# A mixture-of-experts kernel on one core: fixed row regions per expert, a two-part scatter and wide logit products

## What is computed

```python
h = tok(x)                                   # patches @ proj.T + bias + position
h = h + attn(_layernorm(h), ...)             # state-space block
h = h + ffn(_layernorm(h), gate_w, w1, w2, w3, ws1, ws2, ws3)

def ffn(x, ...):                             # T = 1024, D = 192, HID = 512, E = 8, TOP_K = 2
    logits = xf @ gate_w.T
    scores = softmax(logits)
    topk_w, topk_idx = top_k(scores, 2)
    topk_w = topk_w / (topk_w.sum(-1, keepdims=True) + 1e-20)
    cw = zeros((T, E)).at[arange(T)[:, None], topk_idx].add(topk_w)
    y = zeros_like(xf)
    for e in range(E):
        y = y + cw[:, e:e + 1] * _ffn(xf, w1[e], w2[e], w3[e])
    return y + _ffn(xf, ws1, ws2, ws3)       # _ffn(t, a, b, c) = silu(t @ a.T) * (t @ c.T) @ b.T
```

## Time and profile before

| | us |
|---|---|
| three runs, median | 367.04 |
| three runs, lowest and highest | 366.01, 369.85 |
| the profiled execution | 368.0 |
| its span, first to last instruction | 366.3 |

### The profile page before, as it was taken

How to read it: one execution, slowest core, us unless ns; L and a number is a source line. 1 busy time by engine, 2 the same in 40 slices (tenths; PEclk the granted TensorE clock), 3 DMA queues, 4 the chain that set the end, 5 groups by cost and what they waited for, 6 DMA issues and landing times.

```text
span 366.3 us, 6306 instructions
## 1 busy us (share of the span) xinstructions
PE 330.1 (90%) x2042; PEld 270.4 (74%) x2043; DVE 239.3 (65%) x365; ACT 194.1 (53%) x331; POOL 204.2 (56%) x162
## 2 busy tenths in 40 slices
PE   5699979999998788799769999989999999999990
PEld 5653756847876676688668988878888888888870
DVE  1366997989998999999997588864332332223320
ACT  1146993957995666685916649952222222222220
POOL 8120287687896999898875327720333333333332
PEclk9999996999999999899979689999999999999997
DMA  7990820000023320410899999262223322222212
GB/s 188 238 329 17 337 123 2 2 1 5 0 113 118 116 115 4 115 45 2 187 199 233 292 215 236 92 140 70 52 51 52 48 45 45 40 47 50 36 21 22
DMA packets 30184, 37.01 MB, mean 101 GB/s; under 512 B 6112, under 2 KB 26128, under 8 KB 29136
## 3 DMA queue, kind: packets, MB, share of 16 engines
q1 hardware_dynamic: 24160, 30.84, 31.6%
q0 software_dynamic: 4080, 4.39, 7.1%
q10 hardware_dynamic: 1920, 1.46, 1.7%
HBM read 28.29 MB, written 8.40 MB: 100 GB/s over the span
## 4 chain that ended last, share of the span: by engine, by line
PE 34%; DMA 22%; DVE 16%; issue 14%; POOL 7%; ACT 5%; POOLq 1%; SPq 0%; DVEq 0%; ACTq 0%
DMA out<-ysb,token_r 17%; DVE decays L1179 7%; PE ps L1740 6%; POOL rows_scratch L691 5%; PE ps L1694 4%; DMA c_all<-in_xT 3%; ACT decays L836 3%; PE ps L1900 2%; PE ps L1503 2%; POOL states L600 2%; DVE ysb L1410 1%; PE ps L1588 1%; DVE hidden L1095 1%; DVE diagB L1084 1%; PE ps L1534 1%
## 5 line engine op out<-in xcount | busy, mean ns | idle before, releaser
L600 POOL TENSOR_TENSOR states<-decays,c_all 128x1024 f32<-128x1024 f32 x48 | 113.9, 2397 | 19.1 <-DVE decays L1179 19.1
L1179 DVE TENSOR_TENSOR_SCAN decays<-decays,ps 128x1024 f32<-128x1024 f32 x48 | 107.5, 2263 | 3.8 <-PE ps L1694 3.2
L703 POOL DMA_INDIRECT out<-ysb,token_r x23 | 36.1, 1570 | 68.7 <-DVE ysb L1410 57.5
L836 ACT ACTIVATE decays<-dt,negA 128x504 f32<-128x504 f32 (+1 forms) x104 | 62.0, 676 | 7.5 <-POOL states L600 7.4
L956 ACT ACTIVATE sa<-ps 128x512 f32<-128x512 f32 x31 | 18.5, 597 | 80.5 <-PE ps L1866 77.7
L1740 PE MATMUL ps<-ident,states 128*128 128x128 f32 x384 | 55.7, 291 | 4.9 <-POOL states L600 3.5
L1740 PEld LDWEIGHTS ps<-ident,states 128*128 128x128 f32 x384 | 44.1, 148 | 8.9 <-POOL states L600 4.1
L1694 PE MATMUL ps<-diagB,stacked_u 64*128 64x128 f32 x384 | 39.8, 302 | 10.8 <-DVE decays L1179 9.2
L1694 PEld LDWEIGHTS ps<-diagB,stacked_u 64*128 64x128 f32 x384 | 29.5, 194 | 25.1 <-DVE decays L1179 14.8
L1900 PE MATMUL ps<-w,hT 128*128 (+1 forms) x248 | 45.4, 326 | 0.8 <-ACT hT L960 0.8
L1900 PEld LDWEIGHTS ps<-w,hT 128*128 128x128 f32 x248 | 41.8, 190 | 3.5 <-issue 1.0
(11 more groups left out here) (210 smaller groups left out, 589.8 us busy)
## 6 DMA issues: line engine op xcount, KB each, us to landing
c_all<-c_scratch SPq DMA_DIRECT2D x8, 1024.0 KB, 4.7
w_raw<-in_w13T SPq DMA_DIRECT2D x9, 512.0 KB, 11.3
w_raw<-in_w13T SPq DMA_DIRECT2D x18, 256.0 KB, 11.4
w<-in_w2T SPq DMA_DIRECT2D x9, 384.0 KB, 15.5
xs<-rows_scratch SPq DMA_DIRECT2D x23, 128.0 KB, 2.1
...
```

The source lines that it names most:

```text
L600: pool.tensor_tensor(states[:, n % SLOTS, :].rearrange("p (n b s) -> p n b s", n=NH, b=2), decays[:, k % DBUF, t, :, :, :].rearrange("p b ...
L703: pool.indirect_dma_start(out=out_d, out_offset=bass.IndirectOffsetOnAxis(ap=token_r[:, r:r + 1], axis=0), in_=ysb[:, r, :], in_offset=Non ...
L836: return act.activation(decays[:, k % DBUF, tiles[0]:tiles[1], :, n, 1:], dt[g][:, i, tokens].rearrange("p (a b s) -> p a b s", b=2, s=S)[ ...
L1179: dve.tensor_tensor_scan(both, both, unit_banks(n).rearrange("p b n -> p (b n)"), 0.0, ALU.mult, ALU.add).then_inc(scan_ok, 1)
```

## The change

- The scratch has a fixed region of eight tiles for each expert and one spare tile of zeros behind them: 65 tiles instead of 23. A token's row then goes to 1024 times its expert plus its rank, which needs no counts. 17 zero fills instead of 6, of which 11 are issued after the first loads of C.
- Routing and scatter run per group of four tiles: everything from `shifted_logits` to `slots` is done for group 0, then for group 1, and the first eight scatters wait only for group 0. The running sum of group 1 starts from that of group 0. `tile_counts` moves behind step 1 of the loop, `tile_experts` behind step 2, and it now also makes a table `row_tile` of where each routed tile lies.
- SP reads that table to a register before each row load, and the load brings all 260 columns. The `info` load and `slot_weights` are gone; in their place `slot_info` (three instructions of one column behind `x_low`) and `slot_weight` (one behind `gated`) are done for each routed tile. A row buffer is free only when `slot_info` has read it.
- The logits are products with the gate matrix as weights and 512 tokens moving (256 at a time in group 1). The result has experts on partitions; DVE copies it to SBUF (`logits_out`) and PE transposes it back (`logits_by_token`). DVE's copy of group 0 stands before the second group's norm.

```diff
--- before.py
+++ after.py
@@ -45,6 +45,9 @@
 HC = HID // 128
 SLOT_TILES = (2 * T + E * 127) // 128
 TILES = TT + SLOT_TILES
+ROW_TILES = E * TT + 1
+FILLS = -(-ROW_TILES // 4)
...
@@ -66,7 +69,7 @@


         c_d = nc.dram_tensor("c_scratch", [G, 2, TPG, NH, 128], F32).ap()
-        rows_d = nc.dram_tensor("rows_scratch", [SLOT_TILES * 128, ROW], F32).ap()
...
@@ -492,15 +506,21 @@

             sp.wait_ge(zero_ok, 1)
             sp.wait_ge(patch_mm, TPG + 1)
-            for z in range(0, SLOT_TILES, 4):
-                end = min(z + 4, SLOT_TILES)
-                sp.dma_start(rows_v[z:end].rearrange("s p d -> p s d"), zeros[:, 0:end - z, :]).then_inc(zero_st, 16)
+            def fill(z):
+                end = min(4 * z + 4, ROW_TILES)
+                sp.dma_start(rows_v[4 * z:end].rearrange("s p d -> p s d"),
+                             zeros[:, 0:end - 4 * z, :]).then_inc(zero_st, 16)
+
+            for z in range(EARLY_FILLS):
+                fill(z)
             sp.dma_start(sum_v[TT], zeros[:, 0, 0:D]).then_inc(spare_st, 16)
             store_c(0)
             sp.wait_ge(patch_mm, TT)
             sp.wait_ge(c_st[0], 16 * 2)
             for z in range(LOADS):
                 load_c(0, z)
+            for z in range(EARLY_FILLS, FILLS):
+                fill(z)
             store_c(1)
             sp.wait_ge(c_st[1], 16 * 2)
             for z in range(LOADS):
@@ -555,17 +575,20 @@
             def load_rows(n, r):

                 wait(sp, xs_tr, n - 1)
-                sp.dma_start(xs[:, r, :], rows_v[n][:, 0:2 * DA]).then_inc(xs_ld[r], 16)
+                wait(sp, slots_ok, n - 1)
+                at = slice(n, n + 1) if isinstance(n, int) else bass.ds(n, 1)
+                tile = sp.value_load(row_tile[0:1, at], min_val=0, max_val=ROW_TILES - 1)
+                sp.dma_start(xs[:, r, :], rows_p[:, bass.ds(tile, 1), :]).then_inc(xs_ld[r], 16)

             def store_shared(first, end):
                 sp.wait_ge(ysb_ok, end)
                 sp.dma_start(sum_v[first:end].rearrange("s p d -> p s d"), h0[:, first:end, :]).then_inc(y_st, 16)

             EARLY = TT - 2
+            sp.wait_ge(te_ok, 1)
             sp.wait_ge(scat_st, 16 * 2 * TT)
             for n in range(2):
                 load_rows(n, n)
...
@@ -685,16 +707,20 @@
             low_part(pool, BY_POOL - 1)
             pool.wait_ge(low_ok, BY_POOL)

-            pool.wait_ge(pos_ok, 1)
+            pool.wait_ge(zero_st, 16 * FILLS)
             for t in range(TT):
+                if t % TPG == 0:
+                    pool.wait_ge(pos_ok, t // TPG + 1)
                 for k in range(2):
                     pool.indirect_dma_start(
-                        out=rows_d, out_offset=bass.IndirectOffsetOnAxis(ap=pos_i[:, k, t:t + 1], axis=0),
+                        out=rows_d, out_offset=bass.IndirectOffsetOnAxis(
+                            ap=pos_i[:, t // TPG, k, t % TPG:t % TPG + 1], axis=0),
                         in_=xn[:, t, :], in_offset=None).then_inc(scat_st, 16)

             def add_result(n, s, r):

...
@@ -1279,6 +1308,11 @@
                     last = dve.bn_aggr(mv[:, t, :], stats[:, t, :])
                 last.then_inc(aggr_ok, 1)

+            def logits_out(g):
+
+                dve.wait_ge(lgT_mm, g + 1)
+                dve.tensor_copy(lgT[:, GT * g:GT * (g + 1)], ps[0:E, 5 + g, :]).then_inc(lgT_ok, 1)
+
             def read_logits(g):
...
-                chain(dve.tensor_tensor(msum[:, :, 1:].rearrange("p e t -> p t e"), hot[:, 0, :, :], hot[:, 1, :, :],
-                                        ALU.add))
-
-                dve.tensor_tensor_scan(mcum[:, :, :].rearrange("p e t -> p (e t)"),
+                if g:
+                    dve.tensor_copy(msum[:, 1, :, 0], mcum[:, 0, :, TPG])
+                chain(dve.tensor_tensor(msum[:, g, :, 1:].rearrange("p e t -> p t e"), hot[:, g, 0, :, :],
+                                        hot[:, g, 1, :, :], ALU.add))
+
+                dve.tensor_tensor_scan(mcum[:, g, :, :].rearrange("p e t -> p (e t)"),
                                        same_expert[:, :, :].rearrange("p e t -> p (e t)"),
-                                       msum[:, :, :].rearrange("p e t -> p (e t)"), 0.0,
+                                       msum[:, g, :, :].rearrange("p e t -> p (e t)"), 0.0,
                                        ALU.mult, ALU.add).then_inc(mcum_ok, 1)

...
+            def ranks_of(g):
+
+                return ps[:, rank_bank(g), 0:E * (TPG + 1)].rearrange("p (e t) -> p e t", e=E)
+
+            def slots(g):
+
+                dve.wait_ge(rank_mm, g + 1)
+                chain(dve.tensor_tensor(rank[:, g, :, :], ranks_of(g)[:, :, 0:TPG].rearrange("p e t -> p t e"),
+                                        region[:, :].unsqueeze(1).to_broadcast([128, TPG, E]), ALU.add))
+                for k in range(2):
+                    last = dve.tensor_tensor(hot[:, g, k, :, :], hot[:, g, k, :, :], rank[:, g, :, :], ALU.mult)
+                chain(last)
+                chain(dve.tensor_reduce(posf[:, g, :, :], hot[:, g, :, :, :], AX.X, ALU.add))
+                dve.tensor_copy(pos_i[:, g, :, :], posf[:, g, :, :]).then_inc(pos_ok, 1)

             def tile_counts():

-                dve.wait_ge(rank_mm, 1)
-                ranks = ps[:, 4, 0:E * (TT + 1)].rearrange("p (e t) -> p e t", e=E)
-                dve.tensor_copy(rank[:, :, :], ranks[:, :, 0:TT].rearrange("p e t -> p t e"))
-                chain(dve.tensor_copy(cnt[:, :], ranks[:, :, TT]))
+                chain(dve.tensor_copy(cnt[:, :], ranks_of(1)[:, :, TPG]))

                 gt_v = gt[:, :].rearrange("p (e k) -> p e k", k=TT)
                 chain(dve.tensor_tensor(gt_v, cnt[:, :].unsqueeze(2).to_broadcast([128, E, TT]),
                                         steps[:, :].unsqueeze(1).to_broadcast([128, E, TT]), ALU.is_gt))
                 chain(dve.tensor_reduce(ntile[:, :], gt_v, AX.X, ALU.add))
                 chain(dve.tensor_tensor_scan(tend[:, :], ones[:, 0:E], ntile[:, :], 0.0, ALU.mult, ALU.add))
-                chain(dve.tensor_tensor(base[:, :], tend[:, :], ntile[:, :], ALU.subtract))
...
             def tile_experts():


+                ends = tend[:, :].unsqueeze(1).to_broadcast([128, SLOT_TILES, E])
                 chain(dve.tensor_tensor(tcmp[:, :, :], iota[:, :].unsqueeze(2).to_broadcast([128, SLOT_TILES, E]),
-                                        tend[:, :].unsqueeze(1).to_broadcast([128, SLOT_TILES, E]), ALU.is_ge))
+                                        ends, ALU.is_ge))
                 chain(dve.tensor_reduce(tef[:, :], tcmp[:, :, :], AX.X, ALU.add))
+                chain(dve.tensor_tensor(tcmp[:, :, :], tcmp[:, :, :], ends, ALU.mult))
+                chain(dve.tensor_reduce(first_tile[:, :], tcmp[:, :, :], AX.X, ALU.max))
+                chain(dve.tensor_tensor(first_tile[:, :], iota[:, :], first_tile[:, :], ALU.subtract))
+                chain(dve.scalar_tensor_tensor(row_tile_f[:, :], tef[:, :], float(TT), first_tile[:, :],
+                                               ALU.mult, ALU.add))
+                chain(dve.tensor_scalar(row_tile_f[:, :], row_tile_f[:, :], float(ROW_TILES - 1), None, ALU.min))
+                chain(dve.tensor_copy(row_tile[:, :], row_tile_f[:, :]))
                 chain(dve.tensor_scalar(tef[:, :], tef[:, :], float(E - 1), None, ALU.min))
                 dve.tensor_copy(te[:, :], tef[:, :]).then_inc(te_ok, 1)
...
+                dve.wait_ge(te_ok, 1)
+
+            def routed(s):
+
+                return slice(s - TT, s - TT + 1) if isinstance(s, int) else bass.ds(s + -TT, 1)
+
+            def slot_info(s, r):
+
+                n, first = routed(s), xs[:, r, FIRST_EXPERT:FIRST_EXPERT + 1]
                 for k, same in enumerate((ALU.is_equal, ALU.not_equal)):
-                    last = dve.tensor_tensor(chosen[:, k, :], info[:, :, FIRST_EXPERT - 2 * DA], tef[:, :], same)
-                chain(last)
-                for k in range(2):
-                    last = dve.tensor_tensor(chosen[:, k, :], chosen[:, k, :], info[:, :, WEIGHT + k - 2 * DA],
-                                             ALU.mult)
-                chain(last)
-                dve.tensor_tensor(weight[:, :], chosen[:, 0, :], chosen[:, 1, :], ALU.add).then_inc(slots_ok, 1)
-                dve.wait_ge(slots_ok, 1)
+                    dve.scalar_tensor_tensor(chosen[:, k, n], first, tef[:, n],
+                                             xs[:, r, WEIGHT + k:WEIGHT + k + 1], same, ALU.mult)
+                dve.tensor_copy(token[:, n], xs[:, r, TOKEN:TOKEN + 1]).then_inc(slots_ok, 1)
+
+            def slot_weight(s):
+
+                n = routed(s)
+                dve.wait_ge(slots_ok, s + (1 - TT))
+                dve.tensor_tensor(weight[:, n], chosen[:, 0, n], chosen[:, 1, n], ALU.add).then_inc(weight_ok, 1)


             def x_low(s, r):
@@ -1391,12 +1444,16 @@
                     source = ps[:, 4, 0:256].rearrange("p (k n) -> p k n", k=2)
```

(62 more changed lines are left out.)

126 lines of the change are left out of this document (66 added, 60 removed).

## The result

The changed kernel takes 371.33 us (median of 4, 369.62 to 372.75); the kernel before, run on the same chip in turn with it, 366.52. The ratio is 1.0146, 95% interval 1.0095 to 1.0197: slower by 1 to 2%. The forecast of 368.9 was 2.4 us too low; the time is 0.1 us above the upper end of the range that I gave (371.2), which is less than four executions can tell. The ratios leave out executions that took over 1.5% more than the fastest of their kernel, and the medians leave out none, so the two need not agree (one execution with the table spread took 462.3 us). The profiled execution took 371.6 us with a span of 369.8, against 368.0 and 366.3.

The account below looks back on a forecast made before the run. PE's chain of tiles was taken as the bound: its start, interruptions (DVE's list sets both) and 23 routed tiles of 4.79 us. Terms -0.2 + 1.3 - 0.33 + 1.75 - 0.9 + 0.3 = +1.9 gave 368.9 us, range 366.2 to 371.2.

Parts of the forecast that it names:

- Norm 1.8 us later, behind the copy: Ahead of the loop: wide products and DVE's logits copy delay the second group's norm from 202.13 to about 203.9.
- The clock, +1.3: Ahead of the loop: PE's idle 1.4 us before the second ranks lowers the clock for ranks and down, +1.3 us.
- I had -0.2: PE before the loop: the step that started at 216.50 starts at 216.3, -0.2 us.
- Rival B: Ahead of the loop: clock falls in the logits, as before; +2.9 instead of +1.1, total +3.7, 370.7 us; chance 0.18.
- Step 1, -0.33: Behind shared tile 1: counts of about 0.9 us replace the table's 1.18, so PE's stall goes, -0.33 us.
- Step 2, +1.75: Behind shared tile 2: DVE's table, ten chained instructions of 2.74 us, makes PE stand still, +1.75 us.
- The rows' wait, -0.9: Before the first routed transposes: rows lie there before PE asks, so the DMA wait at 243.83 goes, -0.9 us.
- The loop and the end, +0.3: Routed loop: DVE's added one-column instructions make results later, and the last add carries this to the end, +0.3 us.
- The scatter and the zero fills: Scatter beside the shared tiles, done near 235; extra zero fills under the first half of the scan, cost 0.

Follow-up runs that it names:

- table spread: Changed kernel with DVE's ten table instructions spread behind shared tiles 2, 3 and 4 instead of all behind tile 2; 368.94 us, ratio 1.0027 to the kernel before.
- padded gate: Changed kernel with the gate matrix zero-padded to 128 weight columns for the logit products; 371.63 us, ratio 1.0151 to the kernel before.

## Why the prediction was wrong

The direction held, and so did the price of the table. Two terms were far off: what stands ahead of the loop, by 1.4 us, because the loss of the clock was put at the wrong place and too small, and the gain at the rows' wait, by 0.8 us, because it was read from one wait alone. Either miss by itself would have left the time inside the range (370.3 or 369.7); both, with 0.6 us of three smaller ones, did not.

- **Norm 1.8 us later, behind the copy.** Right: from tile 0's first product to the norm it was 3.84 us before and is 5.64. The copy took 0.68 (0.65 estimated).
- **The clock, +1.3.** This is the mis-sized term. I put an idle PE at 212 to 214.5 and let the clock fall behind it, on short products only. The idle time there came (1.30 us at 214.76) and the clock stayed at 1.00 behind it. But I had overlooked that the late norm leaves PE idle once before, between the end of the wide products (202.10) and the first transpose of the second norm (203.16). It stood in my own numbers: products done at 203.2, norm started at 203.9. I wrote that the wide products would keep the clock up through the logits, and did not ask what PE does between the two groups of them. The clock was down from 205.0 to 211.9, and the second logits took 3.8 us instead of 2.1, the half product behind them 2.7 instead of 1.5. In the same order at full clock A was 17.64, and 18.03 with the padded gate, that is -0.6 and -0.2 of before (I had -0.2); with the clock lost it is +2.46. The term is 2.6 to 3.0. Rival B named the place and the size (+2.9 for both), with 0.18 of the chances; the reason that it gave, few columns, is not supported by the padded gate.
- **Step 1, -0.33.** It was -0.15: the counts take less than the table, but the x part still ends 0.2 late.
- **Step 2, +1.75.** +2.00. The ten instructions take 2.83 us with their gaps (230.19 to 233.02; 2.74 estimated, where four times 0.21 had been rounded to 0.80). The spread table gives the 2.03 back in this step.
- **The rows' wait, -0.9.** Wrong: -0.10. The DMA wait did go, and three weight halves of DVE were as late: with what stands between the last half and PE's start in the changed kernel (1.27 us), the kernel before could have gained 0.09. I read one releaser of a place where several chains ended together. The sentence that a thing "lies there before PE asks for it" was true and not enough.
- **The loop and the end, +0.3.** +0.49, but not for the reason given. The 22 routed steps take 0.63 us more (105.48 against 104.85), and what stands behind the last of them takes 0.14 less, so the adds did not carry anything to the end. What lengthens the steps, by 0.03 us each, no run shows.
- **The scatter and the zero fills.** Hidden, as predicted: group 0's scatter began at 214.42 (217.35 before), no wait of PE for a DMA is left there, and the scan stage ended no later (197.11, 198.29 before).

With the terms as measured, +2.46 - 0.15 + 2.00 - 0.10 + 0.49 = 4.7 us, against 1.9. On the median of before that is 371.2 to 371.7, where the kernel is. Rival B's +3.7 and the 0.8 that the rows' wait did not give back are 4.5, the same case. That the time came out at the very edge of the range is chance: an execution with the clock kept has 2.6 to 3.0 us less.
